# Adding the window masks to the local layers' scores by eight small matrix products in place of two or four wide ones

## What is computed

```
q = l2norm(q) * qs;  k = l2norm(k) * ksc;  rotary on both       # 16 heads of 64
bq = q.reshape(b, h, nw, 32, d)                                 # 8 windows of 32 tokens
bk2, bv2 = look(bk), look(bv)                                   # previous and own window: 64 keys
mask = (it < jb) | (it > jb + 32) | (jb == -1)                  # jb == -1: before the first window
sim = einsum('bhwie,bhwje->bhwij', bq, bk2) * 8
sim = where(mask, -finfo.max, sim)
attn = softmax(sim, -1);  out = einsum('bhwij,bhwje->bhwie', attn, bv2)
x = out @ Wo + x;  x = ffn(shift_tokens(x)) + x
```

## Time and profile before

| | |
|---|---|
| device time, median of 3 runs | 2818.03 us (2814.33 to 2821.95) |
| span of the profiled execution | 2820.1 us |
| PE busy | 2481.4 us, 88% of the span |
| DVE, ACT, POOL busy | 2006.5, 1754.3, 1467.4 us |
| local layers | from about 1190 us to the end |
| first and last mask product | 1213.1 and 2759.3 us |

### The profile page before, as it was taken

One profiled execution on the slowest core, in us unless ns is written; L12 is line 12 of the kernel. 1 busy time (PEld: TensorE's weight loads), 2 busy tenths in 40 slices (PEclk: granted clock), 3 DMA queues, 4 the chain that ended last, 5 costly groups with the idle time before them and its releaser, 6 DMA issues. The chain is left out here.

```text
span 2820.1 us, 93390 instructions
## 1 busy us (share of the span) xinstructions
PE 2481.4 (88%) x35216; PEld 1693.3 (60%) x35244; DVE 2006.5 (71%) x3066; ACT 1754.3 (62%) x3659; POOL 1467.4 (52%) x1068
## 2 busy tenths in 40 slices
PE   7999858985647777589999999999999999999994
PEld 4777546664433344246666666666666666766663
DVE  5888653224218888768887888887888887888883
ACT  4666523333216777457777777777777777777773
POOL 2444223222124444366666666666666666666660
PEclk9999969998768999889999999999999999999997
DMA  9100016860410000111111112111211111121110
GB/s 333 35 0 0 20 34 169 233 189 25 132 38 1 0 0 0 53 28 27 26 48 41 39 26 56 34 26 41 58 30 26 48 41 28 37 56 34 26 26 29
DMA packets 124765, 147.61 MB, mean 52 GB/s; under 512 B 12240, under 2 KB 111632, under 8 KB 120336
## 3 DMA queue, kind: packets, MB, share of 16 engines
q1 hardware_dynamic: 120592, 138.22, 18.3%
q0 software_dynamic: 4096, 8.40, 1.0%
HBM read 75.27 MB, written 27.26 MB: 36 GB/s over the span
## 5 line engine op out<-in xcount | busy, mean ns | idle before, releaser
L2372 POOL TENSOR_TENSOR c<-a,bq 128x1024 f32<-128x1024 f32 x192 | 455.0, 2370 | 144.0 <-DVE bq L2437 129.6
L2033 PE MATMUL ps<-wqk,xs 128*128 128x512 f32 x768 | 372.3, 607 | 22.5 <-POOL xs L2365 17.8
L2382 POOL TENSOR_TENSOR qn<-c,ss 128x1024 f32<-128x1024 f32 x192 | 365.2, 1902 | 28.4 <-issue 3.4
L2436 DVE TENSOR_TENSOR a<-ps,tab 128x512 f32<-128x512 f32 x384 | 263.0, 685 | 83.4 <-ACT sq L2209 80.1
L2209 ACT ACTIVATE sq<-ps 128x512 f32<-128x512 f32 x384 | 224.5, 597 | 95.4 <-PE ps L2033 61.2
L2437 DVE TENSOR_TENSOR bq<-ps,tab 128x512 f32<-128x512 f32 x384 | 261.3, 681 | 0.0
L1425 POOL TENSOR_TENSOR hC<-hs,Cs 128x1024 f32<-128x1024 f32 x64 | 150.2, 2352 | 177.6 <-ACT Cs L1570 91.2
L2390 POOL TENSOR_TENSOR z<-z,sm 128x1024 f32<-128x1024 f32 x96 | 182.6, 1902 | 109.8 <-DVE sm L2465 99.1
L2444 DVE TENSOR_REDUCE ss<-sq 128x16 f32<-128x1024 f32 x192 | 230.3, 1199 | 3.9 <-POOL qn L2382 2.4
L2044 PEld LDWEIGHTS ps<-ident,qn 128*128 128x128 f32 x1536 | 173.1, 141 | 78.3 <-POOL qn L2382 40.6
L2033 PEld LDWEIGHTS ps<-wqk,xs 128*128 128x128 f32 x768 | 133.6, 192 | 128.6 <-issue 118.8
(11 more groups left out here) (313 smaller groups left out, 5759.3 us busy)
## 6 DMA issues: line engine op xcount, KB each, us to landing
Ve<-Vo SPq DMA_DIRECT2D x96, 256.0 KB, 4.3
Ve<-Vo SPq DMA_DIRECT2D x96, 192.0 KB, 4.4
win_rows<-rows_q SPq DMA_DIRECT2D x24, 256.0 KB, 3.3
outs_q<-win_out SPq DMA_DIRECT2D x24, 256.0 KB, 2.9
wqk<-in_wqkv SPq DMA_DIRECT2D x6, 1024.0 KB, 5.2
leaves<-in_f_w SPq DMA_DIRECT2D x9, 576.0 KB, 4.3
leaves<-in_q_w SPq DMA_DIRECT2D x1, 4608.0 KB, 18.8
leaves<-in_k_w SPq DMA_DIRECT2D x1, 4608.0 KB, 22.5
```

Of the source, the lines that this page charges most:

```text
L2033: nc.tensor.matmul(jobs.out(n), xs[:, t * 128:(t + 1) * 128], wqk[:, (2 * y + s) * 512:(2 * y + s + 1) * 512], start=True, stop=True).then ...
L2372: nc.gpsimd.tensor_tensor(f(c), f(a), f(bq), ALU.add).then_inc(c_ready.sem, 1)
L2382: nc.gpsimd.tensor_tensor(qn[:, t, y, :, :, :].rearrange("p h s e -> p h (s e)"), c[:, y, :, :, :].rearrange("p h s e -> p h (s e)"), spre ...
L2436: nc.vector.tensor_tensor(a[:, y, :, s, :], Zs, spread(table(0, s), H1), ALU.mult)
```

## The change

The masks are brought in by eight products of 64 rows by 32 columns, the form that the scores have, each of a 32-column piece of the identity by the whole 512-column mask. The edge mask has no product of its own: for `t == 0` the selector of the first window is another matrix (`first_b`), which adds to each query's own mask row the rows 31 and 32; these two together leave the own window open and block the whole previous one. The constants come in one array with the mask, and a semaphore increment stands between the waits and the products.

```diff
-        wmask = sb("wmask", [128, 2 * W])
+        wmask = sb("wmask", [128, 3 * W])
-        first_row, first_mask = sb("first_row", [128, 128], BF16), sb("first_mask", [128, 8, W], BF16)
+        first_b = sb("first_b3", [128, W], BF16)
...
-                nc.gpsimd.memset(first_row[:, :], 0.0)
-                nc.gpsimd.memset(first_mask[:, :, :], 0.0)
-                pool.drain()
-                for p in (0, 64):
-                    nc.gpsimd.memset(first_row[p:p + 1, 0:W], 1.0)
-                    nc.gpsimd.memset(first_mask[p:p + 1, :, :], -1e38)
...
-                nc.vector.tensor_copy(wmask_b[:, :, :], spread(wmask[:, :], 8))
+                nc.vector.tensor_copy(wmask_b[:, :, :], spread(wmask[:, 0:2 * W], 8))
+                nc.vector.tensor_copy(first_b[:, :], wmask[:, 2 * W:3 * W])
...
-                    for j in range(2):
-                        r = slice(64 * j, 64 * j + 64)
-                        nc.tensor.matmul(jobs.out(f"S{t}.{j}"), ident_b[r, :], wmask_b[r, :, :], start=True, stop=False, tile_position=(64 * j, 0))
-                    for j in range(2 if t == 0 else 0):
-                        r = slice(64 * j, 64 * j + 64)
-                        nc.tensor.matmul(jobs.out(f"S{t}.{j}").rearrange("p (h k) -> p h k", k=2 * W)[:, :, W:2 * W], first_row[r, :], first_mask[r, :, :],
-                                         start=False, stop=False, tile_position=(64 * j, 0))
+                    pe.sem_inc(pe_steps, 1)
+                    for w in range(4):
+                        rows = first_b if t == 0 and w == 0 else ident_b[:, w * W:(w + 1) * W]
+                        for j in range(2):
+                            r = slice(64 * j, 64 * j + 64)
+                            nc.tensor.matmul(jobs.out(f"S{t}.{j}")[w * W:(w + 1) * W, :], rows[r, :], wmask_b[r, :, :],
+                                             start=True, stop=False, tile_position=(64 * j, w * W))
...
-                pe.wait_ge(pe_steps, NT * N)
+                pe.wait_ge(pe_steps, 2 * NT * N)
...
+    first = (np.arange(128)[:, None] % (2 * W) == np.arange(W)[None, :]).astype(f)
+    first[[W - 1, W, 3 * W - 1, 3 * W]] += 1.0
```

More of the change, by code:

```diff
@@ L2679, in constants @@
     swapped = (np.arange(128)[:, None] // W) % 2 == 0
-    a["wmask"] = np.where(np.where(swapped, np.roll(seen, W, axis=1), seen), 0.0, -1e38).astype(f)
+    first = (np.arange(128)[:, None] % (2 * W) == np.arange(W)[None, :]).astype(f)
+    first[[W - 1, W, 3 * W - 1, 3 * W]] += 1.0
+    a["wmask"] = np.concatenate([np.where(np.where(swapped, np.roll(seen, W, axis=1), seen), 0.0, -1e38).astype(f), first], axis=1)
     return a
```

## The result

The changed kernel takes 2804.6 us (median of 6 runs, 2802.89 to 2808.65) against 2821.59 (6 runs, 2814.33 to 2825.91) of the kernel before, run beside it: 0.9941 of the time, 95% interval 0.9925 to 0.9957, so 17 us faster (12 to 21). The forecast was 2805.6 us with a gain of 12.4. That the forecast time is met to 1 us is partly luck: the kernel before, run again beside the changed one, has a median 3.6 us above the 2818.03 that the forecast started from, and the gain is 4.6 us larger than forecast; the two nearly cancel. The profiled spans are 2801.1 and 2820.1 us, 19.0 apart.

A forecast was written before the change was run, and what follows sets the result against it. PE, without gaps, was taken to bound the loop. Savings in S1 and S0 gave -0.265 us an iteration, -12.2 us over 46; with outer calls and setup -12.4, so 2818.0 became 2805.6 us, range 2801 to 2814.

The forecast's parts named there:

- PE sets the loop: PE in the local-layer loop has no gap, so a nanosecond off its row is one off the 32.47 us iteration.
- A change of form costs 0.10 us: S1 and S0: the change of tile form between masks and scores goes, -0.10 us in each; the one into masks stays.
- The edge mask's columns: In S0: the edge mask's own two products go, -0.11 us.
- Mask to score 0.24: First mask to first score in S1 and S0: 0.213 us of streaming plus 0.027 for exchanging weights, from 0.31 and 0.43.
- The scores' call unchanged: The score products of S1 and S0: their own time stays at 1.41 to 1.42 us.
- More instructions cost nothing (4): Ten more PE products an iteration in S1 and S0: taken as 0, with 0.11 us of arrival time as bound.
- The increment (5): `pe.sem_inc` and the waits before the masks: taken as 0; without cover some 0.01 to 0.05 us a call.
- the other engines: POOL's `qn` and ACT's `cent`, 0.82 and 0.61 us to spare: neither is reached, with 0.4 us left.
- A: Eight mask places stream bfloat16 only at float32 pace: masks 0.45 us, +7.4 us, 2825.4 us; chance 9%.
- B: Mask places of the same rows wait for each other's weights: masks 0.96 us, +54 us, 2872 us; chance 3%.
- C: Between masks and scores the 0.10 us emptying stays, such as from bfloat16 to float32: -5.5 us, 2812.5 us; chance 12%.
- D: POOL's or ACT's chain takes over through an unseen wait: gain stops at, say, half, -6 us; chance 3%.

The follow-up runs named there:

- Experiments 1: Edge mask folded into the selector, masks left in the wide 64 by 128 form, against the kernel before: iteration 32.37 us, ratio 0.9993.
- 2: Masks as eight products in the scores' form, edge mask kept as two products of its own, against the kernel before: iteration 32.24 us, ratio 0.9967.
- experiment 3: Edge mask folded, masks as four products of 64 by 64, against the kernel before: iteration 32.40 us, one run of 2813.36 us.
- experiment 4: Kernel before with only the semaphore increment added on PE ahead of the mask products: iteration 32.48 us, one time of 2830.37 us.
- 9: Changed kernel with the eight uncut mask products moved behind all 64 score products of a call: iteration 32.16 us, ratio not taken.
- experiment 5: Changed kernel with the mask products reordered, four places of the upper rows, then four of the lower: iteration 32.13 us, one run of 2803.4 us.
- Experiment 6: Changed kernel with each mask product cut into two of 256 columns, 16 products a call: iteration 32.26 us, ratio not taken.

## Why the prediction was right, and where its sizes were off

- **PE sets the loop, and a saving there arrives whole**: right. The iteration fell by 0.35 us, as PE's stages did, and still shows no gap.
- **A change of form costs 0.10 us, and one goes in each call**: right. Experiments 1 and 2 part it from the fold; experiment 3 shows that the form decides, not the width. The 0.53 us from mean to masks stayed, as forecast.
- **The edge mask's columns, 0.11 in S0**: right (32.48 to 32.37 with the fold alone, 32.24 to 32.13 the other way).
- **Mask to score 0.24**: 0.226. The term took an exchange of weights at 0.027, from scores that come right behind a change of form; here the scores' weights were loaded while the masks streamed (loads from 2001.85 us, first score at 2002.05), and 0.013 remained. Twice 0.014 us. The eight masks start within 0.03 us, not the 0.06 that was taken from the scores. The rest of the 0.03 is the 0.31 of S1 before, which is 0.32 without the rounding of its two starts.
- **The scores' call unchanged**: it lost 0.024 us in S1, and as much in S0 together with the stage behind it. Its place in the sum was a plain 0. In the trace the first exchange of weights within the scores falls from 0.08 to some 0.055 us, which is those 0.024: before, the scores came right behind a change of form, with the first weights only then being loaded; now the array is in their form already. The experiments agree: from the first to the last score start it is 1.27 us wherever the scores stand right behind a change of form (before, 1, 3, 4, 9), with 0.08 to the second use of a place, and 1.24 where the eight whole masks are ahead in the scores' form (after, 5, S1 of 2), with some 0.055. No run takes the exchange alone, though: how many scores are ready (32 or 24) changes along with it.
- **More instructions cost nothing (4)**: right in result, and in that partly lucky, since the argument for it (products ahead do not eat into what is ready) does not hold. Experiment 6 prices a further product at 0.0085 us, near the 0.011 of the bound. For the change's own ten it would be 0.085 us an iteration, and that isn't seen. What is seen is that 24 score records, not 32, are ready when the scores start (16 in experiment 6), and that the single ones follow sooner: some 0.19 us after the first start (2034.18 to 2034.37), where it was over 0.25. Why the queue is refilled sooner, and whether this pays for the ten exactly, stays open.
- **The increment (5), the other engines**: right. The loop is 32.48 us with the increment and without (experiment 4), and PE has no gap in the profile after. The 0.01 to 0.05 us that the increment was said to take without cover came from no row, and no run shows it.
- **The rivals**: A (eight places at half pace) and B (places of the same rows in turn) fall by 0.226 us for eight products of 512 columns at the 2.4 GHz level (granted clock 1.00); 512 columns alone are 0.213. The Trainium skill's rule, in "TensorE: Matmul & The Clock Gate", Part 3, The mechanism, that a weight load overlaps only products of another row group, does not hold for this form: the trace disagrees, since the scores' loads start at 2001.85 us while masks stream on all rows, and experiment 5 puts the four places of one row group directly behind each other without a loss. The same section has the load run ahead also where it goes to a background weight buffer; no run here can tell whether that is what happens. C falls too, since bfloat16 masks are followed by float32 scores with no gap, and D, since PE still has no gap.

The mis-sized terms are thus mask to score (0.03 an iteration) and the scores' call (0.05): -0.265 should have been -0.35, which over 46 iterations is the 4 us between -12.4 and about -16. The measured -17 (-12 to -21) holds both; it is the iteration that tells them apart.

## What to carry to other kernels

When small products stand next to work in another tile form, count the changes of form before the columns: here each was 0.10 us, as much as 240 bfloat16 columns, and it goes away by cutting the neighbour into the same form, as long as all its places stream side by side. Folding a second small product into the stationary side of a first cost nothing here and took its columns away; it needs a stationary matrix that can express both. Where many small products follow each other, ask how fast they arrive: eight masks a call in place of two showed no price here, but sixteen in place of eight did, so more but smaller products pay only while they remove something larger.

## What the runs showed of the hardware beyond that

- Eight bfloat16 products of 64 by 32 with 512 columns each run side by side in 0.226 us, four of them on the same rows, in either order.
- Once the queued products are used up, float32 products arrive some 0.017 us apart in the even stretches of a call and bfloat16 ones 0.0085, half. With the pauses between such stretches the 48 float32 products behind the first 16 take 1.00 us in the kernel before, 0.021 each; what makes the pauses stays open. A call of 64 float32 products takes 1.4 us where its columns need 0.85.
- The step from 64*64 tiles of bfloat16 to the scores took 0.02 us more than that from 64*128 (0.34 against 0.32 from mask to score); the step into them cost the same (0.53 from mean).
